# First attention of a fused two-layer kernel: the scaled identity of the next even head made between the two rank adds of a pair

## The chip, the cores and the metric

One NeuronCore of one Trainium2 chip (trn2) runs the whole program. The metric is device time of one execution in microseconds (us), lower is better. PE is the matrix engine (TensorE), DVE the vector engine, ACT the scalar engine, POOL GpSimd, SP the engine that issues most DMAs.

## What is computed

Two layers, each: a conditioning by a two-way recurrence (`_bi_wkv`), an attention, a second conditioning, and a mixture of experts, on x of 4 x 256 x 256. The change lies in the first attention. It has 16 heads of width 16, and logits and probabilities are mixed over the heads, by weights that depend on the token:

```python
def _cross_head_proj(inputs, qw1, qw2, kw1, kw2, qdd, kdd):
    h_q = jnp.einsum('bnts,btin->btsi', inputs, qw1)
    out = inputs + jnp.einsum('btsi,btin->bnts', h_q, qw2)
    h_k = jnp.einsum('bnts,bsin->btsi', inputs, kw1)
    out = out + jnp.einsum('btsi,bsin->bnts', h_k, kw2)
    out = out + inputs * jnp.transpose(qdd, (0, 2, 1))[:, :, :, None]
    out = out + inputs * jnp.transpose(kdd, (0, 2, 1))[:, :, None, :]
    return out
logits = jnp.einsum('bnth,bnsh->bnts', q, k)
logits = _cross_head_proj(logits, pre_qw1, pre_qw2, pre_kw1, pre_kw2, pre_qdd, pre_kdd)
logits = jnp.where(mask, logits, jnp.finfo(jnp.float32).min)
probs = jax.nn.softmax(logits, axis=-1)
probs = _cross_head_proj(probs, post_qw1, post_qw2, post_kw1, post_kw2, post_qdd, post_kdd)
o = jnp.einsum('bnts,bnsh->bnth', probs, v)
```

The mixing has rank 2 on each side. `kw2` of a head scales the columns (s) of two matrices that are the same for all heads (`rankkT`).

## The kernel before

Each engine runs an order written out by hand, and semaphores join them. The first attention goes over 4 batches b. In each, projections come first, then the loop over heads, in pairs (2p, 2p + 1), p = 0 to 7, and a round p = 8 that only finishes the last pair; then a tail in which the mixed parts are turned and multiplied by the values. A head's logits are three blocks of 128 x 128 (one of token tile 0, two of token tile 1), 384 columns in one PSUM bank; the two heads of a pair use banks 0 and 1.

- PE (`scores`, L1593): query-key products of both heads (L1601), the mask (L1604), then for each head a wait for its identities (L1607) and six products of `rankkT` with them (L1610). After that `turn` (L1614) turns the probabilities of the pair before, and `values` (L1623) multiplies them by the values and by ACT's identities of the other side. Every `mm` is recorded at L1519. A 32-bit product shows as two MATMUL records.
- DVE: `diagonals_pre(n)` (L1028, recorded at L1031) makes the identities of head n, four at once: the 128 x 128 identity times a column of `mixw` for each of two ranks and two token tiles, one instruction of 128 x 512, into one of four buffers `diag_pre`. From head 4 on it waits until PE has made the scores of head n - 4, which frees the buffer. `first_rank(n)` (L1006, L1014) adds one rank of the query side to the scores out of PSUM, in two instructions. `maximum(n)` (L1019, L1023) adds the other rank and takes the row maximum, two instructions. `mix(n)` (L1035, L1047; L1045 for head 0) adds the normalised probabilities to the mixed ones, four instructions. `invert(n)` (L1050, L1052) inverts the row sums.
- ACT: `turn_out` (L599) copies turned probabilities, `exps` (L575, L577) makes exponentials and row sums, `second_rank` (L584), `normalise` (L591), and `diagonals_post` (L606), the identities of the other side.
- POOL: `sum_slice` (L445): four adds of 128 x 512 (L448, L449, L452, L453) of the conditioning of another slice. It starts when DVE's `own_term` (L892) has told it, at the end of round p = 5 (the steps of that conditioning are put at the ends of the rounds by `extra`, L1056).

The order on DVE in a round p from 1 to 6: even rank adds, odd rank adds, maximum of the even head, mix of head 2p - 2, maximum of the odd head, reciprocal of the even head, mix of head 2p - 1, reciprocal of the odd head, `diagonals_pre(2p + 2)`, `diagonals_pre(2p + 3)`, the conditioning step. The wait between the two rank adds is

```python
dve.wait_ge(s_read, b * N0 + 2 * p + 1)
```

for DVE's own even rank add. Identities of heads 0 and 1 are made ahead of the loop, those of 2 and 3 within round 0.

## Time and profile before

| | us |
|---|---|
| three runs | 1201.07, 1203.28, 1197.61 |
| median | 1201.07 |
| profiled execution | 1209.78 |
| its span, first to last instruction | 1208.0 |
| mean granted TensorE clock | 0.939 of full speed |

| engine | busy us | share of the span |
|---|---|---|
| PE (products) | 992.7 | 82% |
| PE (weight loads) | 707.7 | 59% |
| DVE | 792.6 | 66% |
| ACT | 599.0 | 50% |
| POOL | 211.3 | 17% |

The head loops of the first attention lie at about 60 to 140, 178 to 258, 299 to 379 and 416 to 495 us. In the rows below "L1014 ... x2" is two instructions of line 1014 merged into one row; the first number is the start, the second the time from the first's start to the last's end. An instruction often starts some 0.07 us before the one ahead of it on its engine has ended. Square brackets give the time for which the engine had been idle, and what ended it.

### The profile page before, as it was taken

What the parts mean: (1) busy time and instruction counts of PE and PEld (TensorE: products, weight loads), DVE (VectorE), ACT (ScalarE), POOL (GpSimd) and SP (SyncE); (2) the same over time, 40 slices, a digit from 0 to 9 for tenths busy, and PEclk for the clock granted to TensorE, in tenths of its full rate; (3) what the DMA queues carried; (4) which work ended last, traced back from release to release, by engine and by line L of the source; (5) the groups of instructions that cost most, each with busy time, mean ns of one, the idle gap of its engine ahead of it and who ended that gap; (6) DMA issues with size and microseconds to landing.
All of it is one profiled execution on the core that took longest, in us unless ns stands there. A gap on an engine that the chain in (4) does not pass through costs nothing.

```text
span 1208.0 us, 18413 instructions
## 1 busy us (share of the span) xinstructions
PE 992.7 (82%) x6320; PEld 707.7 (59%) x6320; DVE 792.6 (66%) x2033; ACT 599.0 (50%) x1452; POOL 211.3 (17%) x179
## 2 busy tenths in 40 slices
PE   0789888988898889689688889689889766999995
PEld 0667666767676667553465666423333254887884
DVE  4568977887788778864188886656766450554452
ACT  3288628862885388431433332246657712544442
POOL 1001020102010201117133333100000022232323
PEclk9999998989999999879899999969999955999998
DMA  9999500000000000034378885425445527577772
GB/s 265 241 229 238 111 1 1 1 1 1 1 2 1 1 1 1 5 112 164 94 247 277 277 277 168 149 89 212 168 178 213 186 68 287 162 205 235 206 238 27
DMA packets 74877, 161.30 MB, mean 134 GB/s; under 512 B 10642, under 2 KB 56990, under 8 KB 70432
## 3 DMA queue, kind: packets, MB, share of 16 engines
q1 hardware_dynamic: 65904, 145.52, 39.4%
q0 software_dynamic: 8880, 14.60, 4.7%
q8 instruction: 51, 0.84, 0.3%
q14 instruction: 42, 0.34, 0.1%
HBM read 127.68 MB, written 62.62 MB: 158 GB/s over the span
## 4 chain that ended last, share of the span: by engine, by line
PE 43%; DVE 20%; DMA 14%; ACT 11%; issue 6%; POOL 2%; another core or an unknown queue 1%; SPq 1%; ACTq 0%; POOLq 0%; DVEq 0%
PE ps L1519 40%; DMA out<-arena 8%; DMA arena<-in_w0all 3%; DVE arena L1047 2%; ACT arena L606 2%; DVE arena L1023 2%; DMA made<-arena 2%; DVE arena L1352 2%; POOL out L507 2%; ACT arena L584 2%; ACT arena L591 1%; DVE arena L985 1%; DVE den L904 1%; ACT arena L599 1%
## 5 line engine op out<-in xcount | busy, mean ns | idle before, releaser
L1519 PE MATMUL ps<-arena 128*128 128x256 f16 (+15 forms) x4712 | 780.3, 341 | 93.3 <-ACT arena L599 29.5
L1519 PEld LDWEIGHTS ps<-arena 128*128 128x128 f32 (+8 forms) x4712 | 531.6, 149 | 270.0 <-issue 111.1
L1503 DVE CAST arena<-arena 128x256 f16<-128x256 f32 x120 | 37.4, 312 | 108.8 <-ACT arena L794 107.1
L1352 DVE TENSOR_REDUCE arena<-ps 128x4 f16<-128x1024 f32 (+1 forms) x48 | 58.8, 1228 | 51.6 <-PE ps L1519 51.6
L448 POOL TENSOR_TENSOR den<-den,backd 128x512 f32<-128x512 f32 x9 | 11.4, 1268 | 430.1 <-DVE euv L892 430.1
L794 ACT ACTIVATE arena<-ps,arena 128x256 f32<-128x256 f32 x120 | 55.8, 474 | 58.2 <-PE ps L1519 57.3
L1047 DVE SCALAR_TENSOR_TENSOR arena<-arena 128x128 f32<-128x128 f32 x240 | 83.7, 411 | 0.5
L606 ACT ACTIVATE arena<-ident,arena 128x128 f32<-128x128 f32 x256 | 80.9, 387 | 0.0
L1014 DVE SCALAR_TENSOR_TENSOR arena<-arena,ps 128x128 f32<-128x128 f32 (+1 forms) x128 | 47.3, 411 | 49.8 <-PE ps L1519 31.2
L477 POOL DMA_INDIRECT made<-arena x47 | 53.0, 1128 | 115.0 <-DVE arena L1265 112.7
L507 POOL DMA_INDIRECT out<-arena x30 | 47.2, 1574 | 144.9 <-DMA out<-arena 84.6
L719 ACT ACTIVATE arena<-ps 128x1024 f32<-128x1024 f32 x48 | 49.2, 1024 | 44.2 <-PE ps L1519 44.2
L904 DVE RECIPROCAL den<-den 128x128 f32<-128x128 f32 x64 | 56.5, 922 | 0.4
L496 POOL DMA_INDIRECT slots<-arena x16 | 15.4, 960 | 230.7 <-DVE arena L1462 226.2
L1505 DVE TENSOR_TENSOR arena<-arena 128x256 f16<-128x256 f32 x120 | 51.1, 426 | 4.1
L591 ACT ACTIVATE arena<-arena 128x128 f32<-128x128 f32 (+1 forms) x128 | 50.3, 440 | 0.0
L1382 DVE TENSOR_TENSOR arena<-arena 128x512 f16<-128x512 f32 x64 | 42.4, 684 | 8.7 <-ACT arena L746 8.7
L584 ACT ACTIVATE arena<-arena 128x128 f32<-128x128 f32 (+1 forms) x128 | 47.3, 441 | 0.0
L1023 DVE CUSTOM_DVE_ANT_0 arena<-arena 128x128 f32<-128x128 f32 (+1 forms) x128 | 47.3, 406 | 0.0
L1519 PE MATMUL ps<-causal,identb 128*128 128x256 bf16 x160 | 36.0, 308 | 13.0 <-DVE arena L1352 10.3
L575 ACT ACTIVATE arena<-arena 128x128 f32<-128x128 f32 x64 | 25.6, 400 | 41.5 <-DVE arena L1023 40.9
L687 ACT ACTIVATE arena<-ps 128x176 f32<-128x176 f32 x47 | 14.9, 318 | 62.6 <-PE ps L1519 57.0
(281 smaller groups left out, 1281.5 us busy)
## 6 DMA issues: line engine op xcount, KB each, us to landing
arena<-split SPq DMA_DIRECT2D x15, 2048.0 KB
arena<-in_w0all SPq DMA_DIRECT2D x47, 608.0 KB
slots<-in_blank SPq DMA_DIRECT2D x17, 1040.0 KB, 16.2
arena<-in_w1all SPq DMA_DIRECT2D x16, 1024.0 KB, 6.7
split<-arena SPq DMA_DIRECT2D x32, 512.0 KB, 3.6
slots<-in_blank SPq DMA_DIRECT2D x9, 1072.0 KB, 19.5
arena<-slots SPq DMA_DIRECT2D x47, 130.0 KB, 3.3
arena<-slots SPq DMA_DIRECT2D x15, 268.0 KB
```

Source lines behind the costliest of these rows:

```text
L477: pool.indirect_dma_start(made0[:], bass.IndirectOffsetOnAxis(ap=ids, axis=0), y0[:, j % Y0N], None, bounds_check=K0 * NT - 1, oob_is_err= ...
L507: pool.indirect_dma_start(out[:], bass.IndirectOffsetOnAxis(ap=ids, axis=0), ytok[:, j % 2, half], None, compute_op=ALU.add).then_inc(adde ...
L584: ins = act.activation(second[:, n % 2, cols], rankq[:, 1, cols], ACT.Copy, scale=mixw[:, tt, 0, 3, n:n + 1])
L591: ins = act.activation(prob[:, n % 3, cols], prob[:, n % 3, cols], ACT.Copy, scale=rinv[:, n % 2, tt:tt + 1])
L606: ins = act.activation(diag_post[:, n % 4, 2 * tt + i], ident[:], ACT.Copy, scale=mixw[:, tt, 3, i, n:n + 1])
L794: act.activation(hfull[:, m], ps[:, m, 0:SLOTS], ACT.Gelu, bias=bias[:, j % 3, 4 * layer + m:4 * layer + m + 1]).then_inc(l_read, 1)
L904: st(dve.reciprocal(part, part))
L1023: ins = dve.tensor_tensor_reduce(logit[:, s, tiles[tt]], logit[:, s, tiles[tt]], second[:, s, tiles[tt]], -1.0, 3.0e38, ALU.add, ALU.min, ...
L1047: ins = dve.scalar_tensor_tensor(dst, prob[:, n % 3, tiles[tt]], w, dst, ALU.mult, ALU.add)
L1352: dve.tensor_reduce(out, ps[:, at:at + 2].rearrange("p j (r s) -> p j r s", r=nr), X, ALU.max, negate=True).then_inc(max1_done, 1)
L1505: st.tell(dve.tensor_tensor(dst[:, 1, m], hfull[:, m], dst[:, 0, m], ALU.subtract), h_split, c + m + 1)
L1519: return pe.matmul(o, l, r, start=start, stop=stop, skip_group_check=shared)
```

## The change

In rounds 1 to 6 `diagonals_pre` of the next even head is issued between the even and the odd rank adds, no longer behind the odd head's reciprocal. That of the next odd head stays where it was, and so do those of heads 0 to 3. The computation is the same.

```diff
                 for p in range(N0 // 2 + 1):
                     if p < N0 // 2:
                         first_rank(2 * p)
+                        if p and 2 * p + 2 < N0:
+                            diagonals_pre(2 * p + 2)
                         dve.wait_ge(s_read, b * N0 + 2 * p + 1)
                         first_rank(2 * p + 1)
                         maximum(2 * p)
...
                     if p < N0 // 2:
                         invert(2 * p + 1)
-                    for n in (2 * p + 2, 2 * p + 3):
-                        if p and n < N0:
-                            diagonals_pre(n)
+                    if p and 2 * p + 3 < N0:
+                        diagonals_pre(2 * p + 3)
                     for step in extra.get(p, []):
                         step()
```

## Rows read from the trace of the kernel before

**Rows 1.** The page's head.
```profile
span 1208.0 us, 18413 instructions
```

**Rows 2.** The chain that ended last, shares of the span by engine.
```profile
PE 43%; DVE 20%; DMA 14%; ACT 11%; issue 6%; POOL 2%; another core or an unknown queue 1%; SPq 1%; ACTq 0%; POOLq 0%; DVEq 0%
```

**Rows 3.** Timeline, a steady pair of batch 2: start, us, engine, line, instruction, idle.
```profile
337.01 0.74 DVE L1014 SCALAR_TENSOR_TENSOR arena<-arena,ps 128x128 f32<-128x128 f32 x2 [0.50 <-PE ps L1519]
...
338.40 0.74 DVE L1014 SCALAR_TENSOR_TENSOR arena<-arena,ps 128x128 f32<-128x128 f32 x2 [0.66 <-DVE arena L1014]
...
339.06 0.28 DVE L1023 CUSTOM_DVE_ANT_0 arena<-arena 128x128 f32<-128x128 f32 x1
...
339.27 0.42 DVE L1023 CUSTOM_DVE_ANT_0 arena<-arena 128x256 f32<-128x256 f32 x1
...
341.61 0.40 ACT L575 ACTIVATE arena<-arena 128x128 f32<-128x128 f32 x1 [0.89 <-DVE arena L1023]
...
342.95 1.27 DVE L1031 TENSOR_TENSOR arena<-ident,arena 128x512 f32<-128x512 f32 x2
...
344.25 2.84 PE L1519 MATMUL ps<-arena 128*128 128x128 f32 x24
...
345.80 0.74 DVE L1014 SCALAR_TENSOR_TENSOR arena<-arena,ps 128x128 f32<-128x128 f32 x2 [0.40 <-PE ps L1519]
```

**Rows 4.** Who waited for L1031 in the whole trace: us, times.
```profile
  PE ps L1519: 3.9, 4
```

**Rows 5.** Timeline of batch 0, rounds p = 6 and 7.
```profile
116.66 0.74 DVE L1014 SCALAR_TENSOR_TENSOR arena<-arena,ps 128x128 f32<-128x128 f32 x2 [1.08 <-PE ps L1519]
116.88 1.28 POOL L449 TENSOR_TENSOR num<-num,backn 128x512 f32<-128x512 f32 x1
...
118.24 1.27 POOL L452 TENSOR_TENSOR den<-den,euk 128x512 f32<-128x512 f32 x1
...
118.71 0.94 DVE L1023 CUSTOM_DVE_ANT_0 arena<-arena 128x128 f32<-128x128 f32 x1
...
119.46 1.31 POOL L453 TENSOR_TENSOR num<-num,euv 128x512 f32<-128x512 f32 x1
...
119.58 1.48 DVE L1023 CUSTOM_DVE_ANT_0 arena<-arena 128x256 f32<-128x256 f32 x1
...
121.10 0.40 ACT L575 ACTIVATE arena<-arena 128x128 f32<-128x128 f32 x1 [1.91 <-DVE arena L1023]
...
124.33 1.26 DVE L1031 TENSOR_TENSOR arena<-ident,arena 128x512 f32<-128x512 f32 x2
...
125.04 2.94 PE L1519 MATMUL ps<-arena 128*128 128x128 f32 x24 [0.98 <-DVE arena L1031]
...
130.50 0.20 ACT L577 ACTIVATION_READ_ACCUMULATOR arena<-arena 128x1 f32 x1
...
131.17 0.16 DVE L1052 RECIPROCAL arena<-arena 128x2 f32<-128x2 f32 x1
...
131.28 0.40 ACT L575 ACTIVATE arena<-arena 128x128 f32<-128x128 f32 x1 [0.59 <-DVE arena L1023]
```

**Rows 6.** Chain in order of time, ends of batches 0, 1 and 3: start, us.
```profile
133.06 3.40 DVE den L904 x4
...
254.83 6.66 PE ps L1519 x20
...
491.64 3.65 PE ps L1519 x20
```

**Rows 7.** Timeline of batch 2, round p = 1.
```profile
304.05 2.94 PE L1519 MATMUL ps<-arena 128*128 128x128 f32 x24
...
306.98 1.51 DVE L1014 SCALAR_TENSOR_TENSOR arena<-arena,ps 128x128 f32<-128x128 f32 x4
...
311.32 0.39 ACT L575 ACTIVATE arena<-arena 128x128 f32<-128x128 f32 x1
```

**Rows 8.** Window us, PE, PEld, DVE, ACT, POOL busy (count), clock, DMA, GB/s.
```profile
255.00:257.00 2.00, 2.00 (x10) 1.04 (x9) 1.97 (x6) 0.00 (x0) 0.00 (x0) 0.50 0.00 0
```

## The prediction, made before the changed kernel was run

> **What bounds the kernel now.** I read the head of the page first: one core, a span of 1208.0 us [rows 1]. The chain that ended last [rows 2] gives 43% to PE, 20% to DVE and 11% to ACT: no engine is the bound by itself, so the stage has to be read for who waits for whom. The change touches only the head loop of the first attention: 4 batches of 16 heads, in pairs p = 0 to 7, plus one round p = 8 that drains.
>
> A steady pair [rows 3] is a ring of three engines, 8.79 us long (rank adds of the even head at 337.01 and at 345.80). PE hands scores to DVE (rank adds L1014, maxima L1023, mixes L1047); DVE hands maxima to ACT (exponentials L575, second ranks, normalising, output-side identities L606, copies of the turned probabilities L599); ACT hands copies back to PE. Each has idle time: DVE 0.50 us ahead of the even rank add and 0.66 us between the even and the odd one, ACT 0.89 us ahead of the odd exponential. The two input-side identities of DVE (L1031, 1.27 us for two) stand at the pair's end; they are finished at about 343.63 and 344.22, and PE's products that read them start at 344.25 with no idle time ahead, the second one's some 1.4 us later still. So in steady pairs nobody waits for an identity. The list of who waited for L1031 says it for the whole kernel: PE matmuls waited for it 4 times, 3.9 us in all [rows 4], once in each batch.
>
> That place is round p = 6, here of batch 0 [rows 5] (the three other batches repeat it within 0.02 us). POOL's four adds for the next conditioning slice, started by L892 at the end of p = 5, run beside DVE. The even maximum (head 12), 0.28 and 0.42 us in a steady pair, takes 0.94 and 1.48; ACT waits 1.91 us for it. DVE comes to its identities late (124.33), PE waits 0.98 us for head 14's identity and starts at 125.04, so it was through its mask products at 124.06. In p = 7 ACT then waits 0.59 us for the odd maximum (head 15). From there the batch ends over DVE in batches 0 and 2 (reciprocals L904) and over ACT and PE in batches 1 and 3 (the last 20 value products) [rows 6].
>
> **The change, part by part.** Nothing is added or removed; 24 identities (even heads 4 to 14, 6 in each of 4 batches) move from the pair's end to the place between the two rank adds. No DMA moves, and no queue of SP or POOL is passed. On DVE the moved instruction is passed by the odd rank add, both maxima, both mixes and both reciprocals, all of which could come later by its time. Its own wait (scores of head 2p - 2 done, which frees the buffer) was met in the pair before, so no new wait arises.
>
> (a) *Ahead of the odd rank add, steady pairs.* The even and the odd adds start 1.39 us apart [rows 3]. The even pair of adds occupies DVE for 0.74 us less some 0.07 of overlap; an identity takes 0.60 (two end in 1.27 at 0.68 each). That is 1.27 us: it fits with some 0.1 us to spare. The profile puts the 0.66 down to DVE's own even add (the wait on s_read), but I take it as PE's: where PE had finished early, in p = 1, four adds with the same wait between them took 1.51 us without a gap [rows 7]. Cost 0; if neither overlaps, 0.74 + 0.68 + about 0.03 is 0.06 us late. The cover is PE's second half of the scores; without it the cost is the whole 0.60.
>
> (b) *p = 1.* There DVE is late and the identity does push the odd add and both maxima by 0.60 (batches 0 to 3 alike). ACT begins the exponentials of head 2 at 311.32, while the maximum of head 2 was ready by about 309.05 (adds from 306.98, 1.51, then the maximum); the work of ACT before it hides 0.60 four times over. Cost 0.
>
> (c) *At the pair's end.* One identity fewer: the odd one and the conditioning step start 0.60 earlier, and DVE idles 1.10 instead of 0.50 ahead of the next even add. In steady pairs worth 0.
>
> (d) *PE's wait at p = 6.* Head 14's identity is made by about 118.1 instead of 124.93, so PE starts its products at 124.06: 0.98 earlier. Late next is head 15's identity, ready at 124.33 + 0.66 = 124.99, needed only after head 14's half (124.06 + 1.4 = 125.5): no wait. Scores, both rank adds and the odd maximum of p = 7 come 0.98 earlier. ACT takes of this only its wait, 0.59. DVE's reciprocal of head 14 (131.17) then waits for ACT's exponential sum (130.50 + 0.20, about 0.06 to get across: 130.76), so DVE gains 0.41.
>
> (e) *POOL at p = 6* [rows 5]. L892 starts 0.60 earlier, and so do POOL's first adds; L449 would end at 116.88 + 1.28 - 0.60 = 117.56. The moved identity of head 14 comes up at about 117.33 and lands beside them. Its cost there is not in the trace. The nearest rows are the two slowed maxima, also with both inputs in SBUF: 0.94 - 0.28 = 0.66 and 1.48 - 0.42 = 1.06 us lost. Each ended as if it had run alone from 0.13 to 0.14 us before the POOL add beside it ended (119.51 and 120.77). The rank adds, one input in PSUM, ran at 0.74 beside POOL. Below, the cost is a gain: if nothing were held, POOL would be out of the way 0.60 earlier and the even maximum with it. Above it is +1.06. I take the rows' own pattern: the identity waits for L449 (to 117.43), runs to 118.03 to 118.11, the odd add starts at 118.05 as before, L452 is held up to the identity's end and ends near 119.23 instead of 119.51, L453 follows, and the even maximum is through 0.28 earlier. ACT, which waits 1.91 for it, gains 0.28.
>
> The Trainium skill, page "SBUF — State Buffer", section "Who interferes with whom", says that a VectorE instruction with two SBUF inputs and a GpSimd instruction that reads SBUF exclude each other for the whole instruction, whoever starts first. By this rule, which speaks against putting the identity there, it is held till L449 ends, and then holds L452; the sum comes out as below. The slowed maxima agree (1.48 us for 0.42), and so does the rank add with an input in PSUM.
>
> **Sum.** ACT: 0.28 + 0.59 = 0.87 a batch (within the 0.98 by which scores are early). DVE: reciprocal of head 14 at 130.76 - 0.28 + 0 = 130.48, which is 0.7 earlier. Batches 0 and 2 end over DVE: 2 x 0.70. Batches 1 and 3 over ACT and PE: 2 x 0.87. Together -3.1 us. The profiled execution took 1209.78 us (1.78 outside its span) and would take 1206.7; it lies 8.71 over the median, so I put the 3.1 on the median: 1201.07 - 3.1 = 1198.0. About 0.5%, 6 us, is what a measurement here can tell from no change (the three runs are 5.67 apart), so this is no change that could be told.
>
> **The rivals.**
> *The identity is held longer beside POOL.* With the whole 1.06 lost the odd add of head 13 comes 117.33 + 0.60 + 1.06 - 118.05 = 0.94 late, and the maxima and ACT with it; head 14's scores still come early, so ACT ends at +0.94 - 0.59 = +0.35 and DVE at +0.94 - 0.41 = +0.53 a batch, 2 x 0.35 + 2 x 0.53 = +1.8: 1202.8. For it: the slowed maxima. Against: a POOL add that is nearly over can't hold it for 1.06. Chance 0.12.
>
> *The odd rank add is late in every pair (slower).* If the 0.66 us is DVE's own after all, as its releaser says, or the identity doesn't overlap, the odd add is late by d, up to 0.60. The ring passes through DVE once in two pairs (from DVE's maximum over ACT to the copies is most of one pair, from there over PE to the scores the next), so it costs d/2 for each of the 20 steady pairs: 20 x 0.30 = 6.0, less 3.1, is +2.9: 1204.0. It outweighs the gain from d = 0.31 on. Against it speak rows 7. Chance 0.08.
>
> *TensorE's clock.* At the end of batch 1 PE ran at a granted clock of 0.50 (the 1.2 GHz level) [rows 8], and the last 20 value products took 6.66 us instead of 3.65 in batch 3 [rows 6]. The change shifts these tails by a fraction of a microsecond to some 3. If that low stretch goes, 3.0 more is gained: 1195.0, and with a second one of the kind more. Chance 0.13. If one comes up elsewhere, 1201.0, no change. Chance 0.15.
>
> *The step does nothing* (POOL takes the 0.28 back and the gain of p = 6 is all there is): 2 x 0.41 + 2 x 0.59 = -2.0, 1199.1; it is counted with the forecast.
>
> **How the numbers follow.** Forecast, with 1199.1 as its weaker end, 0.52; the rivals as above. Only the clock case passes the 6 us on the fast side, and not all of it is sure to: 0.12 faster. Slower by over 6 us needs the late rank add together with a low stretch or a loss beside POOL: 0.07. No change 0.81. The range takes in the forecast and the ends worked out, 1195.0 and 1204.0, and half a microsecond to one and a half for the spread of the runs: 1193.5 to 1204.5.
>
> **What the changed profile would show.** L1031 between the two L1014 groups of a steady pair, their starts still 1.39 us apart, and 8.8 us from pair to pair; over 1.45 apart means the slower rival. No PE wait for L1031 (3.9 us before). At p = 6 an L1031 of 0.7 to 0.9 us that begins near 117.3, L452 up to 0.4 late, ACT's 1.91 down to about 1.6; an L1031 over 1.2 us means the first rival. At p = 7 ACT's 0.59 gone, and DVE waiting some 0.2 for the exponential ahead of L1052. The forecast is wrong if steady pairs get longer or shorter, or if the time moves by more than 6 us without a change in the granted clock.

## The result, and the profile of the changed kernel

The changed kernel takes 1191.3 us at the median of its six runs (1190.51 to 1195.22), the kernel before, in six runs beside it, 1200.86 us (1197.61 to 1203.28). The ratio is 0.992, 95% interval 0.989 to 0.994: faster by 9.6 us, where 3.1 were forecast, and outside the range given. Run again later on other chips it gave 0.994, 0.992 and 0.992. (Of a later run, only_p1to5, one execution of twelve took 1984 us and is left out of its ratio.) The kernel before itself ran at medians of 1200 to 1214 us on these chips, so from here on only ratios to it on the same chip are compared, and stretches within a trace.

The page's head of the profiled execution, to set beside [rows 1]:

```profile
span 1192.4 us, 18413 instructions
PE 993.7 (83%) x6320; PEld 707.5 (59%) x6320; DVE 790.8 (66%) x2033; ACT 599.5 (50%) x1452; POOL 213.1 (18%) x179
```

The work is the same, within 2 us of each engine's busy time; only waits went. Lines behind the edit are one higher than before (the products' line is L1520). Who waited for the identities (L1031), where PE's products had 3.9 us in 4 waits [rows 4] and its weight loads 5.8 us in 8:

```profile
  PEld ps L1520: 0.8, 4
```

Only weight loads still wait, 0.2 us a batch. The pair of [rows 3], p = 4 of batch 2, in the timeline:

```profile
333.87 0.74 DVE L1014 SCALAR_TENSOR_TENSOR arena<-arena,ps 128x128 f32<-128x128 f32 x2 [1.11 <-PE ps L1520]
334.52 0.68 DVE L1031 TENSOR_TENSOR arena<-ident,arena 128x512 f32<-128x512 f32 x1
335.26 0.74 DVE L1014 SCALAR_TENSOR_TENSOR arena<-arena,ps 128x128 f32<-128x128 f32 x2
```

The identity fills the 0.66 us that stood between the two rank adds; they are still 1.39 us apart, and the wait ahead of the even one has grown from 0.50 to 1.11. Rounds p = 6 and 7 of batch 0, for [rows 5]:

```profile
117.92 0.74 DVE L1014 SCALAR_TENSOR_TENSOR arena<-arena,ps 128x128 f32<-128x128 f32 x2 [1.69 <-PE ps L1520]
118.57 0.80 DVE L1031 TENSOR_TENSOR arena<-ident,arena 128x512 f32<-128x512 f32 x1
118.90 1.60 POOL L452 TENSOR_TENSOR den<-den,euk 128x512 f32<-128x512 f32 x1
...
119.31 0.74 DVE L1014 SCALAR_TENSOR_TENSOR arena<-arena,ps 128x128 f32<-128x128 f32 x2
119.97 0.68 DVE L1023 CUSTOM_DVE_ANT_0 arena<-arena 128x128 f32<-128x128 f32 x1
...
120.58 1.48 DVE L1023 CUSTOM_DVE_ANT_0 arena<-arena 128x256 f32<-128x256 f32 x1
...
122.11 0.40 ACT L575 ACTIVATE arena<-arena 128x128 f32<-128x128 f32 x1 [1.65 <-DVE arena L1023]
...
125.15 2.84 PE L1520 MATMUL ps<-arena 128*128 128x128 f32 x24
125.33 0.66 DVE L1031 TENSOR_TENSOR arena<-ident,arena 128x512 f32<-128x512 f32 x1
126.69 0.74 DVE L1014 SCALAR_TENSOR_TENSOR arena<-arena,ps 128x128 f32<-128x128 f32 x2 [0.71 <-PE ps L1520]
...
131.59 0.39 ACT L575 ACTIVATE arena<-arena 128x128 f32<-128x128 f32 x1
131.72 0.17 DVE L1052 RECIPROCAL arena<-arena 128x2 f32<-128x2 f32 x1 [0.47 <-ACT arena L577]
```

PE's wait of 0.98 us is gone, ACT's of 0.59 at p = 7 too, and ACT's wait for the even maximum is 1.65 in place of 1.91. The identity beside POOL took 0.80 us and stretched L452 from 1.27 to 1.60.

From the even rank add of p = 6 to that of the next batch's p = 0 the undisturbed batches 0 to 2 take 62.89 us before and 62.20 after (8.78 + 14.05 + 39.37, against 10.02 + 13.78 + 39.09: to p = 7, to ACT's first copy of the tail L633, to the next batch); the first two parts of batch 3 take 22.85 against 23.81. That is 3 x 0.69 + 0.96 = 3.0 us for the whole kernel. (Batches 0 to 2 gain 0.97 in the first two parts as well and lose 0.28 of it in the third; batch 3 has no such third part, so 3.0 is the upper end of 2.8 to 3.0.) **The head loops gave what was forecast; some 6.6 us came from elsewhere.** The two first profiles can't say from where, since the one of before contains a stall of some 9 us (last section) that its timed runs don't show on this chip.

### The profile page after: what moved, and what is told of

Same layout as the page of the kernel before. It is cut to its first block, busy times and chain, and to the rows that moved or that the text cites. A ratio compares the mean times of both kernels' runs of the same rounds, so it can differ in the third digit from the quotient of the medians.

```text
span 1192.4 us, 18413 instructions
## 1 busy us (share of the span) xinstructions
PE 993.7 (83%) x6320; PEld 707.5 (59%) x6320; DVE 790.8 (66%) x2033; ACT 599.5 (50%) x1452; POOL 213.1 (18%) x179
## 4 chain that ended last, share of the span: by engine, by line
PE 42%; DVE 22%; DMA 14%; ACT 13%; issue 5%; POOL 2%; SPq 1%; ACTq 0%; POOLq 0%; DVEq 0%
PE ps L1520 39%; DMA out<-arena 8%; ACT arena L606 3%; DMA arena<-in_w0all 3%; DMA made<-arena 2%; DVE arena L1047 2%; DVE arena L1023 2%; DVE arena L1353 2%; ACT arena L584 2%; ACT arena L591 2%; POOL out L507 2%; DVE den L904 1%; DVE arena L985 1%; ACT arena L599 1%; ACT arena L577 1%
## 5 line engine op out<-in xcount | busy, mean ns | idle before, releaser
L1520 PE MATMUL ps<-arena 128*128 128x256 f16 (+15 forms) x4712 | 780.6, 341 | 78.8 <-ACT arena L599 29.3
L1520 PEld LDWEIGHTS ps<-arena 128*128 128x128 f32 (+8 forms) x4712 | 531.3, 149 | 254.2 <-issue 105.5
L794 ACT ACTIVATE arena<-ps,arena 128x256 f32<-128x256 f32 x120 | 56.0, 475 | 59.7 <-PE ps L1520 57.6
L1014 DVE SCALAR_TENSOR_TENSOR arena<-arena,ps 128x128 f32<-128x128 f32 (+1 forms) x128 | 47.4, 411 | 48.1 <-PE ps L1520 41.8
L1520 PE MATMUL ps<-causal,identb 128*128 128x256 bf16 x160 | 36.5, 311 | 12.4 <-DVE arena L1353 9.6
## 6 DMA issues: line engine op xcount, KB each, us to landing
slots<-in_blank SPq DMA_DIRECT2D x9, 1072.0 KB, 18.4
```

Source lines behind the costliest of these rows:

```text
L794: act.activation(hfull[:, m], ps[:, m, 0:SLOTS], ACT.Gelu, bias=bias[:, j % 3, 4 * layer + m:4 * layer + m + 1]).then_inc(l_read, 1)
L1520: return pe.matmul(o, l, r, start=start, stop=stop, skip_group_check=shared)
```

## The experiments

Two stretches are compared in all traces. The **attention** runs from the first L1014 of batch 0 to L1129 (hT times its factor, the first step behind the first attention); the **route stage** from there to ACT's L662, behind the shared expert's units. The last column is the route stage less what ACT's waits ahead of its last two L660 take over the usual 2.98 and 2.84 us (a stall of 5 to 11 us in some executions; last section). The expectations count this stage from a memset 2.24 us later: their 57.5 and 55.85 us are 59.8 and 58.1 here.

| kernel | ratio to before, 95% | attention, us | route stage, us | without the stall |
|---|---|---|---|---|
| before, first profile | | 451.24 | 69.07 | 59.8 |
| rep_before | 1.0023 (1.0004 to 1.0041) | 448.11 | 59.79 | 59.8 |
| changed, first profile | 0.9918 (0.9893 to 0.9944) | 446.50 | 58.10 | 58.1 |
| rep_after | 0.9941 (0.9921 to 0.9962) | 444.01 | 58.09 | 58.1 |
| only_p6 | 0.9977 (0.9957 to 0.9997) | 449.79 | 59.77 | 59.8 |
| only_p1to5 | 0.9939 (0.9918 to 0.9959) | 443.84 | 58.09 | 58.1 |
| after_late | 1.0009 (0.9988 to 1.0031) | 447.41 | 67.67 | 58.1 |
| before_warm | 0.9975 (0.9958 to 0.9991) | 454.37 | 65.05 | 59.7 |
| early14 | 0.9961 (0.9935 to 0.9987) | 446.49 | 64.14 | 58.1 |
| after_warm | 0.9955 (0.9933 to 0.9977) | 446.40 | 66.07 | 60.8 |
| after_c2 | 0.9919 (0.9888 to 0.9950) | 443.51 | 69.35 | 58.1 |
| after_late2 | 0.9997 (0.9967 to 1.0028) | 447.47 | 69.33 | 58.1 |
| before_fill | 0.9910 (0.9876 to 0.9943) | 446.82 | 67.46 | 59.7 |
| after_fill | 0.9949 (0.9922 to 0.9975) | 450.00 | 69.60 | 59.7 |
| after_c3 | 0.9918 (0.9887 to 0.9950) | 443.47 | 58.10 | 58.1 |
| after_trim | 0.9894 (0.9863 to 0.9925) | 440.31 | 60.59 | 60.6 |
| before_trim | 0.9870 (0.9844 to 0.9896) | 440.22 | 58.10 | 58.1 |
| before_trimend | 0.9949 (0.9929 to 0.9969) | 448.96 | 58.09 | 58.1 |
| after_trim2 | 0.9919 (0.9887 to 0.9950) | 440.61 | 60.58 | 60.6 |
| before_trim2 | 0.9911 (0.9879 to 0.9942) | 442.66 | 58.09 | 58.1 |

Four groups of runs each had their own chip: rep_before to only_p1to5, after_late to after_warm, after_c2 to after_fill, after_c3 to before_trimend; the last pair ran on the chip of the fourth group. In the expectations, theory A is that of the prediction, theory B that something outside the head loops counts. The kernel before against itself, rep_before, came out at 1.0023 with an interval that leaves out 1: a difference of 0.2 to 0.3% between two rows of the table says nothing. Behind the route stage comes the second half of the program, which takes 618.8 to 629.9 us in these profiles (625.3 at the mean of before, rep_before and before_warm, 626.1 at that of the six of the changed order named below). It is as variable as the first half and was not followed up; the profiles show no gain there.

**Both kernels again, and the change in two halves.** rep_before and rep_after are the two kernels unchanged.

> The kernel before, unchanged, against itself. Theory A (the change is worth what its two waits at p = 6 and p = 7 are, about 3 us, and the rest of the 9.6 us between the medians is chance or the particular profile): ratio within 0.2% of 1, and a profile whose last shared units of the experts (L660) have no waits of 7 us. Theory B (something in the old order costs several us outside the head loop, each time): the two waits of 7.9 and 7.2 us ahead of L660 near 575 and 583 us are there again. The head loop itself should repeat: 10.0 us from the even rank add of p = 6 to that of p = 7, four times.

> The changed kernel again. Theory A: 3 to 5 us under the kernel before (0.996 to 0.9975). Theory B: 8 to 10 us under it (0.992), and no waits over 3 us ahead of L660. Both: 8.77 us from the even rank add of p = 6 to that of p = 7.

only_p6 moves head 14's identity alone, only_p1to5 those of heads 4 to 12:

```
                         first_rank(2 * p)
+                        if 0 < p < 6:                  # only_p1to5; only_p6: if p == 6
+                            diagonals_pre(2 * p + 2)
                         dve.wait_ge(s_read, b * N0 + 2 * p + 1)
...
-                    for n in (2 * p + 2, 2 * p + 3):
-                        if p and n < N0:
-                            diagonals_pre(n)
+                    if p and not (0 < p < 6) and 2 * p + 2 < N0:   # only_p6: if p and p != 6 and ...
+                        diagonals_pre(2 * p + 2)
+                    if p and 2 * p + 3 < N0:
+                        diagonals_pre(2 * p + 3)
```

> Only the identity of head 14 is moved between the rank adds (round p = 6), one in each batch; the five others of a batch stay at the pair's end. Theory A: the gain of the whole change except the 0.28 us of the earlier POOL adds, since those start from the end of round 5, which is as before: ACT waits 1.9 us for the even maximum or more, 0.59 of p = 7 gone, 2.0 us in all. If the identities of the steady pairs matter (rival), it gains clearly less than the changed kernel, by more than 2 us.

> The identities of heads 4 to 12 are moved (rounds 1 to 5), that of head 14 stays at the end of round 6, where PE waits for it. Theory A: POOL's adds start 0.60 earlier and nothing delays them, so the even maximum of p = 6 is 0.6 earlier (ACT waits 1.3 instead of 1.9); PE's wait for L1031 stays near 1 us; in all 1 to 2.4 us under the kernel before. If the steady pairs were what counts: as much as the changed kernel, 9 us.

The split that I expected of these two was wrong, though the forecast of the whole was right. From p = 6 to the next batch, only_p6 takes 62.80 us, 0.09 less than before (0.37 less in batch 3), so 0.6 in all, not 2.0; only_p1to5 takes 62.30, 0.59 less in each batch (0.60 in the last), 2.4 in all. The timeline of only_p6, batch 0, shows why:

```profile
118.09 0.74 DVE L1014 SCALAR_TENSOR_TENSOR arena<-arena,ps 128x128 f32<-128x128 f32 x2 [1.07 <-PE ps L1522]
...
118.75 1.41 DVE L1031 TENSOR_TENSOR arena<-ident,arena 128x512 f32<-128x512 f32 x1
...
120.07 0.73 DVE L1014 SCALAR_TENSOR_TENSOR arena<-arena,ps 128x128 f32<-128x128 f32 x2
...
122.88 0.40 ACT L575 ACTIVATE arena<-arena 128x128 f32<-128x128 f32 x1 [2.25 <-DVE arena L1023]
```

Here L892 is not earlier, POOL's second add L449 (118.32 to 119.60) still has most of its time to go, and the identity is held for 0.73 us: 1.41 in place of 0.68. The odd rank add comes 1.98 us behind the even one, ACT waits 2.25 in place of 1.91. That is the mechanism of the first rival (0.73 lost, where it had 1.06), and it eats nearly all that PE's lost wait brings. In only_p1to5 the identity of head 12 no longer stands ahead of L892, POOL's spell comes 0.60 us earlier, and ACT waits 0.59 less:

```profile
120.89 0.40 ACT L575 ACTIVATE arena<-arena 128x128 f32<-128x128 f32 x1 [1.32 <-DVE arena L1023]
```

Only with that does head 14's identity meet the end of L449 and take 0.80. But by its time only_p1to5 is as fast as the whole change: 0.9939, or 7.3 us, where its loops give 2.4. Its attention is 5.8 us shorter than the mean of the first two profiles of before, its route stage 1.7 shorter. The head loops' waits do not hold that difference. What differs beside them in the rows is TensorE's granted clock.

**Where the clock falls.** The end of batch 1 in windows of 1 us, first in the first profile of before, then in rep_before, the same program (columns: window, its length, busy time of PE, PEld, DVE, ACT and POOL with instructions, granted clock, DMA share, GB/s):

```profile
253.00:254.00 1.00, 0.46 (x3) 0.22 (x3) 1.00 (x2) 1.00 (x5) 0.00 (x0) 1.00 0.00 0
254.00:255.00 1.00, 0.17 (x2) 0.17 (x4) 0.96 (x2) 0.77 (x3) 0.00 (x0) 0.62 0.00 0
255.00:256.00 1.00, 1.00 (x8) 0.38 (x6) 0.96 (x3) 0.00 (x0) 0.00 (x0) 0.50 0.00 0
```

```profile
253.00:254.00 1.00, 0.48 (x3) 0.24 (x3) 1.00 (x2) 1.00 (x5) 0.00 (x0) 1.00 0.00 0
254.00:255.00 1.00, 0.15 (x2) 0.14 (x4) 0.96 (x2) 0.80 (x3) 0.00 (x0) 1.00 0.00 0
255.00:256.00 1.00, 1.00 (x10) 0.59 (x7) 0.96 (x3) 0.00 (x0) 0.00 (x0) 1.00 0.00 0
```

Activity is the same to 0.03 us, within 0.1 us of the same time in the trace; once the clock falls to 0.50 (the 1.2 GHz level) and the batch's end (p = 7 to L633) takes 16.78 us, once it stays at 1.00 and it takes 13.79. The low stretches before it begin at the same times too (73.3 and 189.4 us, 73.3 and 189.3). So the fall comes behind a spell of little work on PE, but what decides whether it comes is finer than these rows show.

The place of the low stretches is not tied to the program's start: in the six profiles of the changed order (the first, rep_after, after_c2, after_c3, early14, after_warm) the first one of batch 0 begins 9.97 to 11.44 us behind the first rank add, although the kernels are the same up to there. The Trainium skill, page "TensorE: Matmul & The Clock Gate", section "Part 1: The HAM clock gate", says that the window in which activity is judged runs freely and does not start with the kernel; these six profiles agree.

The second place is p = 1, whose 28 value products follow three waits of PE. In rep_before's batch 1, then the same row of after_c2:

```profile
186.56 0.55 PE L1619 MATMUL ps<-ident,arena 128*128 128x128 f32 x3 [0.70 <-ACT arena L591]
188.42 0.55 PE L1619 MATMUL ps<-ident,arena 128*128 128x128 f32 x3 [1.31 <-ACT arena L591]
190.34 7.29 PE L1519 MATMUL ps<-arena 128*32 128x256 f32 x28 [1.37 <-ACT arena L599]
```

```profile
189.65 6.03 PE L1520 MATMUL ps<-arena 128*32 128x256 f32 x28 [1.36 <-ACT arena L599]
```

At full clock the 28 take 4.49 us, in both kernels. A stretch of low clock begins in all four batches of both (the 28 then take 5.9 to 6.1 us); in some a second one follows (7.3 to 7.6 us, and p = 0 to p = 2 takes 19.8 to 20.0 us in place of 18.4 to 18.7). It costs 1.2 to 1.4 us. All three profiles with the order of before and nothing filled in the attention (before, rep_before, before_warm) have it at batch 1, before_warm at batch 2 too; of the six with the changed order (the first, rep_after, after_c2, after_c3, early14, after_warm) three have it once, at batch 0, and three not at all. The end of a batch took 16.78 us once in before, 15.20 and 16.83 in before_warm, 15.67 in the first changed profile and 15.68 in after_warm. The attention took 451.2 us at the mean of those three and 445.1 at that of those six: 6.2 apart, of which the head loops are 3.0 and such stretches the rest. With the route stage's 1.7 it makes 7.9, near the measured 7 to 10 (0.9918 to 0.9941 of some 1200 us). The spread within the three is as large as the difference, so these means alone would not carry it.

**What decides the second stretch at p = 1.** The trace holds the start of every stretch of low clock. In the 14 profiles with nothing filled at p = 1, counted from each batch's first rank add:

| the first stretch begins | batches | a second one follows | p = 0 to p = 2 |
|---|---|---|---|
| 9.78 to 10.30 us behind it | 13 | in all 13 | 19.8 to 20.0 us |
| 10.35 to 11.99 us behind it | 43 | in none | 18.4 to 18.7 us |

Where no extra stretch comes between, these first stretches stand 116.05 us apart (rep_after: 74.97, 191.02, 307.08, 423.13 us). A batch of the changed kernel without extra stretches takes 115.9 to 116.2 us, so the distance hardly moves from batch to batch, and if it is right in batch 0 it stays right. One of the kernel before takes 116.6 to 116.9, so the distance shrinks by 0.6 to 0.8 us a batch: 10.44, then 9.83 in the first profile of before, 10.35, then 9.78 in rep_before, and batch 1 has the second stretch. So the 0.69 us of the change did more than shorten a batch: they brought its length to the spacing of the stretches. This is read off programs that were made for other questions; the delay below bears it out, but no run was made for it.

**The clock of the timed executions.** The mean granted clock of every execution is on record, without a profile. It was 0.9396 for before and 0.9465 for the changed kernel in the first group, 0.9335 and 0.9420 in the third, 0.9370 and 0.9453 in the fourth. Among the executions of the kernel before alone, on one chip, 0.01 less goes with 6 to 11 us more (correlation -0.68 to -0.82 in five sets). By that the changed kernel's clock is worth 4 to 9 us: an estimate from a correlation, in the size of the 6.6 us that are looked for, and from all executions and not from single profiles.

**A delay that has nothing to do with identities.**

```
                         dve.wait_ge(h_done, b * N0 + n)
+                    if n == N0 - 1:
+                        for s in range(2):
+                            dve.tensor_scalar(logit[:, s], logit[:, s], 1.0, None, ALU.mult)
```

> The changed kernel with two idle VectorE instructions (128x384, in place on a dead tile, about 0.3 to 0.4 us each) ahead of the last mix of each batch, where PE's tail waits for them: each batch gets back what the change took from it (about 0.7 us, 2.8 in all), by a delay that has nothing to do with the identities. Theory A (the change is worth its three us in the head loops and nothing outside them; medians differ further by chance): 1192 + 2.8 = 1195. Theory B (the later stages come out cheaper or dearer by the moment at which they are entered, since the stretches in which TensorE's granted clock is 0.50 fall elsewhere): the low stretch at 530 to 535 comes back with the old moment of entry, the shared stage takes 57.5 us again instead of 55.85, and the median goes to 1198 to 1201. Theory C (something in the identities' own order, apart from any time, matters outside): the shared stage stays at 55.85 and the median at 1195.

> The changed kernel once more, as the partner of the delayed one on the same chip. Its three profiled and twelve timed executions so far stand at 0.992 to 0.994 of before; the same is expected here, 0.993 (0.991 to 0.995), under every theory. Where the profile shows no extra stretch of granted clock 0.50 in the attention batches the span is the shortest.

> The changed kernel with two idle VectorE instructions ahead of the last mix of each batch, run beside the changed kernel without them. The trace of the first run of it shows the delay as 0.54 us per batch (2.2 us in all) and nothing else in the head loop. Theory A (times add up: a delay costs itself): 2.2 us over the changed kernel, ratio to before 0.995. Theory B (where later stages are entered decides how much of them falls into stretches of low clock): the loss is a multiple of the delay, 5 to 10 us, ratio to before 0.998 to 1.002, as the first run of it gave (1.0009).

The timeline of after_late2 shows the delay ahead of the last mix of batch 0:

```profile
139.47 0.63 DVE L1042 TENSOR_SCALAR arena<-arena 128x384 f32<-128x384 f32 x2
```

It makes each batch 0.54 us longer, 2.2 in all. The time went from 0.9919 to 0.9997 of before on one chip, 7.5 us between the medians: **the whole gain was gone**, with the identities still in their new place. Theories A and C fall. The mean granted clock fell with it, from 0.9420 to 0.9302, under that of the kernel before (0.9335). (Theory B's detail, that the route stage would be long again, was wrong: it took 58.1 us.) The trace shows part of it: a batch takes 116.7 us again, as before the change, the distance goes from 10.81 to 10.18 us in after_late and from 10.90 to 10.30 in after_late2, and batch 1 of both, on two chips, has the same second low stretch as before,

```profile
190.91 7.55 PE L1523 MATMUL ps<-arena 128*32 128x256 f32 x28 [1.37 <-ACT arena L599]
```

and the attention is 3.96 us longer than after_c2's for 2.2 us of delay. The profiled executions stand 5.6 us apart (1210.70 and 1205.06), of which some 1.7 lie behind the route stage; the rest of the 7.5 is in no profile of mine.

**Filling TensorE's waits.** If low stretches make the difference, it should go when PE has no waits ahead of them. The fills are products of the identity by itself, results unused:

```
+                def fill(bank, count):
+                    for _ in range(count):
+                        mm(ps[:, bank, 0:P], ident[:], ident[:])
+
...
                     if p:
+                        if p == 1:
+                            fill(2, 4)                      # trimmed: 3
                         turn(2 * p - 2)
+                        if p == 1:
+                            fill(3, 8)                      # trimmed: 5
+                        if p == N0 // 2:
+                            pe.wait_ge(t_read, b * N0 + 14)
+                            fill(3, 7)                      # trimmed: 4
                         turn(2 * p - 1)
+                        if p == 1:
+                            fill(4, 9)                      # trimmed: 5
+                        if p == N0 // 2:
+                            pe.wait_ge(s_read, b * N0 + N0)
+                            fill(0, 9)                      # trimmed: 5
                         values(p - 1)
```

before_fill and after_fill have the first counts, before_trim and after_trim the trimmed ones; before_trimend has the trimmed ones at the end of the head loop alone.

> The kernel before with idle matmuls (128x128, identity by identity, 0.13 us each) in the waits of TensorE at p=1 (4, 8 and 9 of them in waits of 0.71, 1.31 and 1.36 us) and at the end of each batch's head loop (7 and 9 in waits of 1.05 and 1.36 us), so that it is not idle just before the places at which the granted clock fell. Theory B: the extra stretches of clock 0.50 there (at the end of batch 1 in one profile, at the start of batch 1 in both, 1.2 to 3 us each) go, and the regular one after p=1 shrinks or goes (up to 1.2 us per batch): 5 to 9 us under before, 0.993 to 0.996. Theory A (the clock has no part in the difference): the fills only cost where they overrun, 0 to 1 us over before.

> The changed kernel with the same idle matmuls. If the clock makes the part of the difference that the head loops do not (theory B), the two filled kernels stand only the 3 to 4.7 us apart that both traces show as fixed, not 7 to 9.6: with before_fill at 0.994, this at 0.990 to 0.991. By theory A they stand as far apart as the kernels without fills (0.992 to 0.994 of each other).

> The changed kernel with fewer idle matmuls, since each 128x128 one of 4-byte numbers showed as two records of 0.12 us, 0.24 us together, and the first fills overran (0.9 to 1.6 us per batch at the end of the head loop): now 3, 5 and 5 at p=1 and 4 and 5 at the end, 0.7 to 1.2 us each. Clock theory: p=0 to p=2 takes 17.8 us as with the first fills, p=7 to L633 14.0 to 14.3, so 0.5 to 0.8 us per batch under the changed kernel, and no extra low stretch: 2 to 4 us under the changed kernel, ratio 0.989 to 0.991. If the fills bring low stretches at other places (as after_fill's two at the ends of batches 0 and 1), no gain: 0.993.

> The kernel before with the same trimmed fills. The first, overrunning fills already gave 0.991. Clock theory: the extra low stretches go and nothing overruns, p=7 to L633 takes 13.8 to 14.0 us instead of 14.64: 0.988 to 0.991 of before; against after_trim it stands 3 to 5 us higher, the part of the change that needs no clock. If the 0.991 was of another origin: 0.994 to 0.998.

> The kernel before with the trimmed fills at the end of the head loops alone (4 and 5), none at p=1. It tells which extra stretches the difference lies in. If in those at the batch's end (one of three profiles of the kernel before shows one at 254.5 us that cost 3 us; the wait of TensorE for L1031 at p=6, which the change removes, lies 10 us ahead of it): 0.993 to 0.995 of before. If in those after p=1 (all three show one to two, 1.3 us each): 0.998 to 1.0.

> The changed kernel as the partner of the filled ones on this chip. Pooled from the earlier runs: 0.992 to 0.994 of before. The mark at the first attention's end lies 443.5 to 444.5 us behind the first rank add if no extra stretch of low clock falls into the attention, 1.2 to 3 us later for each that does.

With fills the kernel **before** ran at 0.991 of itself, as fast as the changed kernel on the same chip (0.992; medians 1205.77 and 1205.72 us), and, trimmed, at 0.987, faster than it (1186.26 against 1191.46 us), with the identities where they were. The expectation for after_fill failed: 0.9949, not 0.990 to 0.991. Its fills overran by 1.57 us in every batch (p = 7 to L633 takes 15.62 in place of 14.05; 0.87 in before_fill), and low stretches came up at the ends of batches 0 and 1 (17.15 and 17.30 us). So before_fill against after_fill is no fair pair.

Trimmed, neither kernel overruns there (13.77 and 14.05 us). Batch 1 in the trace of before_trim, against rep_before's above:

```profile
188.49 1.28 PE L1519 MATMUL ps<-ident 128*128 128x128 f32 x10
190.02 4.49 PE L1519 MATMUL ps<-arena 128*32 128x256 f32 x28 [0.25 <-ACT arena L599]
```

p = 0 to p = 2 takes 16.96 us in all four batches of both trimmed kernels, 1.6 less than the usual 18.60 and 1.4 less than the best without fills, and no extra stretch comes at the batch's end. before_trimend came out at 0.9949, as the first of its two expectations had it: by its time the waits at the batches' ends hold 0.5% of the 1.3% that all trimmed fills give, more than the extra stretches there come to in the profiles of before (3.0, 0 and 4.5 us in three). Its own trace has two extra stretches at p = 1 (19.85 and 19.82 us), where nothing was filled. But the fills also take away the stretch that every batch of both kernels has at p = 1, so only filled against filled speaks of the change. I expected before_trim to stay 3 to 5 us above after_trim. It did not: it stands at 0.987 against 0.989, and the intervals overlap. The fills had made the changed kernel's p = 1 just as short (16.96), and its loops still hold their 0.69 us per batch; but a low stretch now lies elsewhere. Ten turns (L1575) and the 32 rank products of batch 1, first after_trim, then before_trim:

```profile
164.28 5.20 PE L1575 MATMUL ps<-ident,arena 128*128 128x128 f32 x40 [1.86 <-DVE arena L970]
171.30 7.01 PE L1520 MATMUL ps<-arena 128*128 128x128 f32 x32 [1.82 <-DVE arena L985]
```

```profile
163.43 6.25 PE L1574 MATMUL ps<-ident,arena 128*128 128x128 f32 x40 [1.85 <-DVE arena L970]
170.56 5.47 PE L1519 MATMUL ps<-arena 128*128 128x128 f32 x32 [0.88 <-DVE arena L985]
```

In before_trim the stretch comes in this batch alone and lies on the turns, which then only shorten PE's next wait from 1.8 to 0.9. In after_trim it lies on the rank products, which DVE and ACT wait for, in all four batches (it begins at 54.99, 171.04, 287.09 and 403.15 us, 116.05 apart, and a batch takes 116.04): 1.5 us each (L633 to the next batch's first rank add takes 40.88 us in place of 39.36). The same waits, begun 0.85 us apart, and the stretch costs next to nothing or 6 us. So a batch as long as the spacing repeats a bad place as well as a good one.

**The last pair** adds six fills in the 1.86 us ahead of the turns to both trimmed kernels:

```
                 tokens0(b, 1)
+                fill(5, 6)
                 for u in range(10):
```

> after_trim with six more idle matmuls (1.5 us) in TensorE's 1.86 us wait ahead of the ten turns of each batch. In after_trim's trace a low stretch follows that wait and lies on the rank products (7.0 us in place of 5.5, so 1.5 us per batch on the chain, all four batches); in before_trim's it follows the same wait three us earlier and lies on the turns, which are covered. Clock theory: without the wait no stretch, 40.89 us from L633 to the next batch's first rank add becomes 39.1 to 39.4, 6 us less than after_trim in all: 0.984 to 0.986 of before. If it comes back elsewhere on the chain: 0.989.

> before_trim with the same six matmuls. Its stretch at 164 us is covered, so it should stay at 0.987 (0.985 to 0.989). If both kernels are now free of stretches on the chain of the attention, they differ by the head loops alone: after_trim2 2.5 to 3.5 us below before_trim2, as the traces' 0.69 (0.96 in the last batch) per batch say. If the identities' order were worth the whole 8 to 9 us by itself, after_trim2 would stand that far below.

Both expectations failed: 0.9919 in place of 0.984 to 0.986, and 0.9911 in place of 0.987, so that the six fills took back part of what the trimmed ones had given the kernel before. In after_trim2 the stretch stayed on the rank products in batches 1 to 3, behind the other wait of 1.82 us (row below), and one came up in before_trim2, ahead of batch 2, as well.

```profile
159.64 1.56 PE L1520 MATMUL ps<-ident 128*128 128x128 f32 x12
161.67 5.20 PE L1580 MATMUL ps<-ident,arena 128*128 128x128 f32 x40 [0.47 <-DVE arena L970]
168.69 7.13 PE L1520 MATMUL ps<-arena 128*128 128x128 f32 x32 [1.82 <-DVE arena L985]
```

So neither kernel was ever wholly free of them, and "the fixed 3 us alone" was not shown by a time. What the pair does show: 0.9919 and 0.9911, where the unfilled kernels differ by 0.8%. The intervals are 0.3% wide to each side, so this excludes the 0.8%, not the 3 us (0.25%) of the head loops, which the traces show in the filled kernels too.

**The route stage.** Without the stall it takes 59.7 or 59.8 us in before, rep_before, only_p6, before_warm and before_fill, and 58.1 in all eight unfilled kernels that have the changed order or most of it, the delayed ones among them. Windows 525 to 535 of rep_before, then rep_after:

```profile
525.00:530.00 5.00, 2.76 (x9) 1.12 (x8) 4.08 (x17) 3.43 (x6) 0.00 (x0) 1.00 0.00 0
530.00:535.00 5.00, 5.00 (x13) 2.34 (x12) 4.14 (x20) 0.00 (x0) 1.09 (x1) 0.66 0.01 3
```

```profile
525.00:530.00 5.00, 3.67 (x13) 2.11 (x14) 3.73 (x18) 0.51 (x1) 0.00 (x0) 1.00 0.01 3
530.00:535.00 5.00, 5.00 (x13) 2.26 (x12) 4.66 (x14) 1.20 (x2) 3.49 (x4) 1.00 0.15 53
```

So among unfilled kernels these 1.7 us come with the change each time, a delay of 2.2 us or not. But they don't hang on the identities' order: before_trim and before_trimend have the old one and take 58.1, after_fill and after_trim the new one and take 59.7 and 60.6. It is how the stretches lie against the stage. In rep_before the clock rose again at 523.9 us, 12.8 behind the stage's start, the products ahead of the selection were through early, PE waited 2.2 us for it, and the clock fell once more at 530.7; in rep_after it rose 14.4 us behind the start, the wait was 1.5 us, and it did not fall. All 20 profiles follow this: in the seven in which the clock rises 11.8 to 13.5 us behind the start it falls again at 18.7 to 20.3, and the stage takes 59.7 to 60.6 us; in the thirteen in which it rises 13.9 us behind the start or later it does not, and the stage takes 58.1, but for the two below whose added products overran. Why the old order, unfilled, mostly brings the early rise was not settled. Two tries to remove these stretches by products of their own:

```
+            pe.wait_ge(route_dve, 1)                        # before_warm, ahead of the wait for the selection
+            for _ in range(4):
+                mm(ps[:, 0], shgu[:, 0, 0:P], hT[:, 0, 0:512], True, True)
+            for _ in range(48):                             # after_warm, ahead of the route product
+                mm(ps[:, 6, 0:P], ident[:], ident[:], True, True)
```

> The kernel before with four added matmuls (128x512 each, about 0.45 us, results unused) in the 2.2 us in which TensorE waits for the selection in the route stage (527.4 to 529.6 us in the trace of the kernel before run again). Theory B: TensorE stays busy, the stretch of granted clock 0.50 to 0.66 at 530 to 535 us goes, the shared stage takes 55.9 us instead of 57.5, and the median is 1.7 us under the kernel before, about 1199. Theory A: the low stretch has nothing to do with that wait; the stage stays at 57.5 us and the median within 0.5 us of before.

> The changed kernel with 48 added matmuls (128x128, identity by identity, results unused) on TensorE between the last batch's output product and the route product, where it idles 5 us (503 to 510 us) and after which its granted clock is 0.50 until 522 us. Theory B: the clock is 1.00 or nearly so in the route stage, route product and turns take about half of their 7.0 and 3.6 us, of which at least the route product's 3.5 us lie in the chain: 3 to 5 us under the changed kernel, 1188. If the low stretch is not set by TensorE's idling there, the time stays at 1192 or rises by what the matmuls overrun.

Both overran, since each such product is two records (below): 4 x 0.87 = 3.5 us in a wait of 2.2, and 48 x 0.24 = 11.5 us in one of 5. before_warm's stage stayed at 59.7 us, after_warm's grew to 60.8. In before_warm the clock rose 14.1 us behind the start and did not fall again, but since a late rise alone goes with that, the added products can't be given the credit. before_warm's 0.9975 has no explanation in its trace, whose attention is the longest of all. As tests of the route stage's clock both are inconclusive.

**Head 14's identity a round earlier**, at the end of p = 5, out of POOL's way (and no longer between the rank adds of p = 6):

```
                     if p and 2 * p + 3 < N0:
                         diagonals_pre(2 * p + 3)
+                    if p == 5:
+                        diagonals_pre(14)
```

> The changed kernel with head 14's identity made at the end of round p=5 instead of between the rank adds of p=6, where GpSimd's slice step holds it and the even maximum. By the trace: in p=6 VectorE has 0.80 us less ahead of the odd rank add, so L452 and the even maximum come that much earlier against GpSimd, ACT's wait for the maximum of 1.65 us shrinks to 0.9 to 1.3, and each batch gains 0.3 to 0.7 us more: 1190 to 1191 at the median if the stages behind stay as they are. Rival: at the end of p=5 the identity delays the slice step (L892) and head 12's rank add by 0.68 us, GpSimd's spell falls wholly on p=6's maxima, and nothing is gained or 0.3 us per batch are lost (1193).

No gain by the trace; the changed kernel itself was not run on that chip, so 0.9961 has no partner. The identity now stands ahead of L892 again, POOL's spell is 0.6 us later, ACT's wait for the even maximum is 1.92 us as before the change, and p = 7 to L633 takes 14.32 in place of 14.05: 0.3 us per batch lost, which is the rival of the expectation. That fits only_p6: what counts at p = 6 is when L892 starts.

## Why the prediction was wrong

*Step (a), steady pairs cost nothing: right.* 1.39 us between the adds, pairs of 8.78 and 8.90 us in all traces. *Steps (b) and (c): right*, nothing is seen of them at full clock; the wait of 1.10 us that (c) forecast is 1.11.

*Steps (d) and (e): right for the change as a whole.* The forecast was 0.70 us in batches 0 and 2 and 0.87 in 1 and 3, together 3.1; the traces have 0.69 in batches 0 to 2 and 0.96 in the last, together 3.0. ACT's 1.91 came down by 0.26 to 1.65 (forecast 0.28), its 0.59 at p = 7 went, L452 was held by 0.33 (up to 0.4), PE's wait is gone; only DVE's wait ahead of L1052 is 0.47 where some 0.2 were forecast. What was wrong is what I expected of the halves, as if the terms stood by themselves. Head 14's identity alone gives 0.09 to 0.37, not 0.41 to 0.59, since POOL holds it if L892 isn't earlier; the five others alone, which make L892 0.60 earlier, give 0.59 where the identity does not stand in POOL's way. That they would was in (e), as its lower bound.

*The step that failed is the rival "TensorE's clock"*, and behind it the words "the change shifts these tails by a fraction of a microsecond to some 3". It was priced as one stretch at one place (the end of batch 1, 3.0 us, chance 0.13) and balanced by a new one elsewhere (0.15), so that nothing was left of it in the expected time. The runs show in its place: stretches at p = 1 of every batch, at the ends of batches, in the batch's projections and in the route stage, each worth nothing to 3 us by what it lies on; one to four extra ones in the attention of a profile of before, none to two in one of the changed kernel; and a shift of 0.54 us per batch moved the time by 7.5 us, nearly as much as the change. At p = 1 it is not a matter of one hit or miss, as the rival had it: a second stretch goes with the place of the first in the batch, that place moves from batch to batch by the batch's length less 116.05 us, and the change altered just that length, in every batch. That the rest of the 9.6 us does not belong to the identities' order is shown by the delay (the gain goes with the identities in place) and by the two trimmed pairs (the orders are then equal within intervals that leave out the 0.8%, though low stretches still fell differently in the two). That it is the clock is what the rows of the attention and the route stage show, 7.9 us with the head loops, and the clock of the timed executions. How the 6.6 us divide among the places is not: single profiles differ by as much as the kernels do (the three of before by 6.3 us in the attention), and before_trimend alone speaks of places, giving the ends 0.5% of 1.3%.

The second failing is in how the sum was used. A change of 3 us was set against a median whose executions, of one program, lie 12 us apart (1194.6 to 1207.0 in 29 runs), and their mean clock with them (0.932 to 0.944). The range of 11 us took in what I had priced, not what a shift can do to a kernel that lives on both clock levels.

## What to carry to other kernels

Where an engine's clock follows its activity, the time of a kernel is not the sum of its waits: before crediting a reordering with a gain, run it with a plain delay that gives the saved time back, and run the old kernel with the bound engine's short waits filled. Here the second of these beat the change: before_trim, 0.987, though six fills more took it back to 0.991. In a loop, compare the length of a round with the spacing of the low stretches: if the two agree, each round repeats what the first one got. And of a step beside GpSimd, look at what starts GpSimd: moving that start by 0.6 us was worth 0.6, moving the visible wait hardly 0.1.

## What the runs showed that I had not expected

The clock fell to 0.50 behind waits of 0.70, 1.31 and 1.37 us with work between them, in every batch that had no fills there. At the end of batch 1 it fell or did not with the same activity.

Each 128x128 product of 4-byte numbers is two records of 0.12 us (ten records in 1.28 us for five products, above), a 128x512 one two of 0.43. Whoever counts fills by records halves them.

ACT waited up to 10 us longer for its last shared unit in some executions, though PE's products and DVE's mixes for it had ended. after_c2, then rep_after:

```profile
575.11 0.59 ACT L660 ACTIVATE arena<-ps 64x512 f32<-64x512 f32 x1 [12.80 <-remote]
```

```profile
565.22 0.59 ACT L660 ACTIVATE arena<-ps 64x512 f32<-64x512 f32 x1 [2.84 <-PE ps L1520]
```

The wait is 7.2 to 12.8 us long in the first profile of before (there twice) and in all eight profiles of the second and third group, whatever the kernel, and in none of the others; on those two chips the kernel before had its highest medians (1209 and 1214 us). The view calls the releaser "remote"; nothing in the traces says what is waited for, and I made no run for it.
